# The first tile of rows for a mixture of experts: turned by TensorE from marks of the slots, with later row loads and turns moved within a tile

## The reference

```python
h = (x - mu) * jax.lax.rsqrt(var + LN_EPS) * ln_g + ln_b
logits = jnp.einsum('btd,ed->bte', h, w_r) + b_r
topk_vals, topk_idx = jax.lax.top_k(logits, K)          # K = 2 of 8
gates = jax.nn.softmax(topk_vals, axis=-1)
hid = jax.nn.gelu(jnp.einsum('nd,edf->nef', hf, W1) + b1, approximate=False)   # 512 -> 2048
expert_stack = jnp.einsum('nef,efd->ned', hid, W2) + b2                        # 2048 -> 512
# each row: its two experts' results, weighted by the gates, added to x
```

## Time and profile before

| what | value |
|---|---|
| time, median of 3 runs | 2133.72 us (2128.21 to 2137.45) |
| the profiled execution | 2126.98 us, of which 2125.2 us span |
| TensorE busy | 1715.3 us, 81% |
| VectorE, ScalarE, GpSimd busy | 919.6, 519.3, 875.1 us |
| granted TensorE clock, mean | 0.935 |

### The profile page before, as it was taken

How to read it: one execution, slowest core, us unless ns; L and a number is a source line. 1 busy time by engine, 2 the same in 40 slices (tenths; PEclk the granted TensorE clock), 3 DMA queues, 4 the chain that set the end, 5 groups by cost and what they waited for, 6 DMA issues and landing times. The chain is left out here.

```text
span 2125.2 us, 27922 instructions
## 1 busy us (share of the span) xinstructions
PE 1715.3 (81%) x8075; PEld 1126.1 (53%) x8076; DVE 919.6 (43%) x2223; ACT 519.3 (24%) x1459; POOL 875.1 (41%) x1032
## 2 busy tenths in 40 slices
PE   4649988756937777786879999279999999999992
PEld 4224434334436666652434465157777777777770
DVE  3852266344159999969845638400000000000001
ACT  0011101111138888820111122011222211122220
POOL 0677778777669999965011100220000000043002
PEclk9999998978969999998889999589999999999996
DMA  7900031000230000010210013543803320420003
GB/s 202 298 2 2 2 76 31 2 2 2 65 114 25 0 0 0 0 61 0 94 56 1 0 37 122 211 131 150 331 20 144 150 76 20 178 63 20 20 20 102
DMA packets 77073, 150.32 MB, mean 71 GB/s; under 512 B 19795, under 2 KB 21402, under 8 KB 72802
## 3 DMA queue, kind: packets, MB, share of 16 engines
q1 hardware_dynamic: 50533, 125.26, 16.5%
q0 software_dynamic: 19200, 11.30, 3.7%
q10 hardware_dynamic: 7294, 13.21, 1.8%
HBM read 111.35 MB, written 37.99 MB: 70 GB/s over the span
## 5 line engine op out<-in xcount | busy, mean ns | idle before, releaser
L310 POOL DMA_INDIRECT sorted_edges<-fa_records,fa_edge_slot x320 | 399.4, 1248 | 176.2 <-issue 176.2
L1838 PEld LDWEIGHTS et_ps_h<-et_turned,arena 128*128 128x128 f32 x3072 | 348.6, 193 | 19.2 <-issue 15.9
L1838 PE MATMUL et_ps_h<-et_turned,arena 128*128 128x128 f32 x3072 | 349.1, 276 | 7.6 <-issue 4.5
L1847 PE MATMUL et_ps_y<-arena,et_hidden_t 128*128 x768 | 333.6, 592 | 0.0
L909 POOL TENSOR_SCALAR ad_row<-iota,ad_row_no 128x128 fp32r<-128x128 f32 x354 | 237.9, 685 | 0.1
L1847 PEld LDWEIGHTS et_ps_y<-arena,et_hidden_t 128*128 128x128 f32 x768 | 144.0, 190 | 172.2 <-issue 172.2
L1749 POOL DMA_INDIRECT xn_rows<-slot_out,slots x10 | 12.2, 1218 | 493.8 <-POOLq L1746 491.0
L986 PE MATMUL ad_ps_w<-ad_to,ad_row_high 128*128 128x320 f32 x472 | 150.1, 330 | 63.5 <-POOL ad_row_low L914 60.5
L964 ACT ACTIVATE ad_row_high<-ad_row,ad_edges 128x128 fp32r<-128x128 f32 x472 | 184.5, 391 | 67.9 <-DVE ad_row L933 67.0
L1765 DVE COPY et_turned<-et_ps_t 128x512 f32<-128x512 f32 x25 | 17.3, 692 | 370.7 <-PE et_ps_t L1819 370.7
L931 DVE TENSOR_SCALAR ad_to<-iota,ad_edges 128x320 fp32r<-128x320 f32 x472 | 176.6, 433 | 0.0
(11 more groups left out here) (363 smaller groups left out, 2327.2 us busy)
## 6 DMA issues: line engine op xcount, KB each, us to landing
arena<-L_ffn_W SPq DMA_DIRECT2D x16, 4096.0 KB, 13.3
slot_rows<-fa_zeros SPq DMA_DIRECT2D x1, 7424.0 KB
slot_out<-fa_zeros SPq DMA_DIRECT2D x1, 6912.0 KB
et_rows_in<-slot_rows ACTq DMA_DIRECT2D x26, 256.0 KB, 2.6
slot_out<-et_y ACTq DMA_DIRECT2D x24, 256.0 KB, 2.0
sorted_edges<-fa_records,fa_edge_slot POOLq DMA_INDIRECT x320
x_in<-x SPq DMA_DIRECT2D x1, 2500.0 KB
neighbour<-fa_Wv SPq DMA_DIRECT2D x10, 250.0 KB
```

What stands on the lines that cost most here:

```text
L310: nc.gpsimd.indirect_dma_start(g.sorted_edges, bass.IndirectOffsetOnAxis(ap=self.edge_slot[0:NT, e:e + 1], axis=0), self.records[0:NT, e, ...
L1838: last = pe.matmul(ps_h[:, f % 2, i, :], x.weights[:, at:at + P], turned[:, k, :], start=(k == 0), stop=(k == KD - 1))
L1847: last = pe.matmul(ps_y[:], hidden_t[:, i, :], x.weights[:, bass.ds(buffer * (2 * HALF) + (HALF + i * D), D)], start=(i == 0), stop=(i == ...
```

## The change

It has three parts.

**Early and late scatters.** One list of twenty scatters, lower slots first. POOL issues the first seven (EARLY = 7) in nodes and does not wait for them; it issues the other thirteen in expert_tiles, behind the announcement of expert 0. All count on one semaphore, `rows_scattered`.

**The first tile without DRAM.** In nodes VectorE makes `marks`: for each node tile a 125x128 matrix with a 1 where a row's lower slot equals the column's number. TensorE multiplies the rows by the marks, 4 x 10 matmuls into one PSUM bank, which gives the rows of slots 0 to 127 turned. ScalarE copies the bank to `x.turned`, which lives on into expert_tiles (and holds the row `be` before that, whose buffer is dropped). No load, turn or copy of tile 0 is left in expert_tiles; TensorE gives the three semaphores their first counts there.

**Loads and turns in the loop.** ScalarE's queue loads the rows of tile t + 1 behind the Gelus of tile t, and TensorE turns them ahead of the last quarter of tile t's second product instead of ahead of its first.

```diff
+EARLY = 7
+def scatter_rows(nc, g, choices):
+    for i in choices:
+        n, t = divmod(i, T)
+        nc.gpsimd.indirect_dma_start(
+            g.slot_rows, bass.IndirectOffsetOnAxis(ap=g.slots[0:NT, n, t:t + 1], axis=0),
+            g.xn[0:NT, t, :], None).then_inc(g.rows_scattered, 16)
...
+        marks = sums[:, 2 * DST - T * P:].rearrange("p (t n) -> p t n", t=T)
...
@@ nodes, gpsimd
             pool.wait_ge(s["slots_ready"], 1)
-            for t in range(T):
-                nc.gpsimd.indirect_dma_start(
-                    g.slot_rows, bass.IndirectOffsetOnAxis(ap=g.slots[0:NT, 0, t:t + 1], axis=0),
-                    g.xn[0:NT, t, :], None).then_inc(g.rows_scattered, 16)
-            pool.wait_ge(g.rows_scattered, 16 * T)
+            scatter_rows(nc, g, range(EARLY))
@@ nodes, scalar
+            act.wait_ge(s["first_turned"], 1)
+            nc.scalar.copy(x.turned[:].rearrange("p k n -> p (k n)"), banks[:, 3, :])
@@ nodes, vector
+            c.link(v.tensor_tensor(least[r, :], chosen_slot[0][r, :], chosen_slot[1][r, :], ALU.min))
+            for t in range(T):
+                v.tensor_scalar(marks[r, t, :], g.iota[r, 0:P], column(least, t), None, ALU.is_equal).then_inc(s["marked"], 1)
@@ nodes, tensor
+            for k in range(KD):
+                for t in range(T):
+                    if k == 0:
+                        pe.wait_ge(s["marked"], t + 1)
+                    last = pe.matmul(banks[:, 3, k * P:(k + 1) * P], g.xn[r, t, k * P:(k + 1) * P], marks[r, t, :],
+                                     start=(t == 0), stop=(t == T - 1))
+            last.then_inc(s["first_turned"], 1)
@@ expert_tiles, gpsimd
             announce(0)
-            for t in range(T):
-                nc.gpsimd.indirect_dma_start(
-                    g.slot_rows, bass.IndirectOffsetOnAxis(ap=g.slots[0:NT, 1, t:t + 1], axis=0),
-                    g.xn[0:NT, t, :], None).then_inc(g.rest_scattered, 16)
+            scatter_rows(nc, g, range(EARLY, 2 * T))
@@ expert_tiles, vector
-            move_turned(0)
@@ expert_tiles, scalar
-            load_rows(0)
-
-            act.wait_ge(s["rows_turned"], 1)
-            act.wait_ge(g.rest_scattered, 16 * T)
-            load_rows(1)
...
-                act.wait_ge(s["rows_turned"], t + 2)
-                load_rows(t + 2)
+                act.wait_ge(g.rows_scattered, 16 * 2 * T)
+                act.wait_ge(s["rows_turned"], t + 1)
+                load_rows(t + 1)
@@ expert_tiles, tensor
-            turn_rows(0)
+            for n, amount in (("rows_loaded", 16), ("rows_turned", 1), ("rows_ready", 1)):
+                pe.sem_inc(s[n], amount)
...
-                turn_rows(t + 1)
                 pe.wait_ge(s["weights_ready"], e * 2 + 2)
                 pe.wait_ge(s["y_out"], t + 1)
                 for f in range(FC):
                     pe.wait_ge(s["hidden_ready"], t * FC + (f + 3))
+                    if f == FC - 1:
+                        turn_rows(t + 1)
```

More of the change, by code:

```diff
@@ L424, in __init__ @@
         self.scattered, self.rows_scattered = m.sem("scattered"), m.sem("rows_scattered")
-        self.rest_scattered = m.sem("rest_scattered")
         self.low_gathered, self.gathered = ([m.sem(f"{n}{t}") for t in range(T)] for n in ("low_gathered", "gathered"))
@@ L1005, in __init__ @@
         self.weights = arena
-        self.b1 = m.sb("b1", [P, EXPERTS * FT])
+        self.b1, self.turned = m.sb("b1", [P, EXPERTS * FT]), m.sb("turned", [P, KD, P])
         self.ends = m.sb("ends", [P, EXPERTS], I32)
@@ L1122, in nodes @@
         agg = m.sb("agg", [P, 2, GCN])
-        be = m.sb("be", [P, D])
+        be = x.turned[:].rearrange("p k n -> p (k n)")
         in_degree, degree, positive, guess, root_y, root_off = (
@@ L1147, in nodes @@
                  "q_ready k_ready dotted comp_in comp_ready agg_done agg_out value_ready out_done out_taken h_ready lifted rows_made "
-                 "logits_done picked counted odds_in odds2_ready slots_ready "
+                 "logits_done picked counted odds_in odds2_ready slots_ready marked first_turned "
                  "chain")
@@ L1183, in _ @@
             sp.dma_start(expert, A["L0_ffn_We"][bass.ds(e, 1)].squeeze(0).rearrange("(k p) n -> p k n", p=P)).then_inc(s["fetched"], 16)
-            sp.dma_start(be[:], A["L0_ffn_be"][bass.ds(e, 1)].squeeze(0).partition_broadcast(P)).then_inc(s["fetched"], 16)
+            sp.dma_start(be, A["L0_ffn_be"][bass.ds(e, 1)].squeeze(0).partition_broadcast(P)).then_inc(s["fetched"], 16)
             load_matrix(sp, wo, A["L1_mix_Wo"], s["rest_in"])
@@ L1687, in expert_tiles @@
         m = Memory(nc, stack, "et_")
-        turned, hidden_t = m.sb("turned", [P, KD, P]), m.sb("hidden_t", [P, FT, P])
+        turned, hidden_t = x.turned, m.sb("hidden_t", [P, FT, P])
         rows_in, y = m.sb("rows_in", [P, D]), m.sb("y", [P, D])
@@ L1741, in _ @@
             pool.wait_ge(s["weights_ready"], 2 * EXPERTS)
-            pool.wait_ge(g.rest_scattered, 16 * T)
+            pool.wait_ge(g.rows_scattered, 16 * 2 * T)
             low_end = pool.value_load(x.ends[0:1, EXPERTS - 2:EXPERTS - 1], min_val=0, max_val=SLOT_TILES)
@@ L1779, in load_rows @@
             def load_rows(t):
-                act.dma_start(rows_in[:], in_rows[t] if isinstance(t, int) else in_rows[bass.ds(t, 1)].squeeze(0)
-                              ).then_inc(s["rows_loaded"], 16)
-            load_rows(0)
-            act.wait_ge(s["rows_turned"], 1)
-            act.wait_ge(g.rest_scattered, 16 * T)
-            load_rows(1)
+                act.dma_start(rows_in[:], in_rows[bass.ds(t, 1)].squeeze(0)).then_inc(s["rows_loaded"], 16)
             with used_tiles(act) as t:
@@ L1804, in _ @@
             act.sem_inc(s["finished"], 1)
-            act.wait_ge(s["rows_loaded"], last_end(act) * 16 + 32)
+            act.wait_ge(s["rows_loaded"], last_end(act) * 16 + 16)
             act.sem_inc(s["finished"], 1)
```

## The result

The changed kernel took 2105.49 us (median of 4 runs, 2102.89 to 2111.30), the kernel before, run with it on the same chip, 2130.97 us (4 runs, 2123.45 to 2137.45). The ratio is 0.9888, with an interval of 0.9853 to 0.9923: 1.1% faster. A later series of 6 runs gave 2110.83 against 2129.17 (11 runs), 0.9906 [0.9877, 0.9934]. The forecast was 2116 us. Its profiled execution took 2105.39 us with a span of 2103.6, so 21.6 us less than the span of the profile before.

The account below looks back on a forecast made before the run. TensorE bounds the loop without idle time but stands almost still for 37 us ahead of it. Hand-over 14.4 plus first-tile stall 3.1 gives 17.5 us, from the 2133.72 median 2116 us, range 2106 to 2126.

Parts of the forecast that it names:

- The base: Whole kernel: 17.5 us gain measured from the runs' median, 2133.72 us, the profiled execution being 6.7 us faster.
- Early scatters: End of nodes: POOL's drain holds until seven scatters land; B, the barrier's opening, at 1374.0 to 1375.0 us, taken as 1374.5.
- the first rival: End of nodes: POOL's drain doesn't hold; TensorE and the copy set B at 1371.3, gain 20.8 us, 2113 us; chance 0.13.
- The entry: Start of expert_tiles: first pass at B + 5.4, between B + 4.2 and B + 6.8, with 0.7 us per register load.
- Marks and forty matmuls: In nodes: ten marks 3 us, matmuls from 1358.3 to 1369.2 or 1371.0; hidden by POOL, 2 to 4 us to spare.
- Both rivals about them: In nodes: clock stays at half, gain 14.7 us, chance 0.06; marks hold up scatters, gain 14.5 us, chance 0.07; each 2119 us.
- ScalarE at B: First tile: ScalarE enters its loop when the barrier opens, removing the wait before the third quarter; 3.1 us gained.
- Late scatters: First tile: thirteen land at B + 26.9, tile 1's rows loaded at B + 29.5, wanted at B + 32.2; 2.7 us to spare.
- The loop: Loop: loads 3 us and turned rows about 2 us to spare; seams bounded at 0.2 us a tile, taken as nothing.
- The slower rival: Loop: the turn in the last quarter misses each next tile's start; at 1.2 us late each, 2145 us; chance 0.04.

Follow-up runs that it names:

- e5: Changed kernel plus twenty more marks on VectorE into spare buffers, beside the early scatters; 2113.0 us (one run).
- e8: Changed kernel with EARLY = 6 and the turn ahead of the last three of sixteen blocks instead of the last four; 2109.57 us (one run).
- e3: Changed kernel with ten early scatters instead of seven (EARLY = 10); 2122.4 us.
- e6: Changed kernel with a semaphore wait on POOL for the seven early scatters, ahead of the drain at the end of nodes; 2105.02 us.
- e9: Kernel before, with its late scatters held until the first quarter of the first product is done; 2142.64 us.
- e4: Changed kernel with three early scatters instead of seven (EARLY = 3); 2108.28 us.
- e1: Kernel before with only the changes in the loop, none at the hand-over; 2122.76 us (8 runs), ratio 0.9966 to the kernel before.
- c1: Kernel before, traced once more without a change; 2127.77 us.
- e2: Changed kernel's hand-over with the loop of the kernel before; 2131.32 us (10 runs), ratio 1.0004 to the kernel before.
- c2: Changed kernel, traced once more without a change; 750.7 us from S, the start of the slots instruction, to the end.
- e10: Changed kernel with EARLY = 5 and the turn ahead of the last three of sixteen blocks; 2106.08 us (6 runs), ratio 0.9892 to the kernel before.
- e7: Changed kernel with 28 unread matmuls (twelve ending nodes, sixteen starting expert_tiles) in TensorE's gap; 755.2 us from S, the slots instruction's start, to the end.

## Why the prediction came out as it did

The mechanism is the forecast's: POOL's drain holds the barrier, nothing in the loop is lost, and the gain is in the hand-over and the first tile. The gain was 18.9 and 19.9 us behind S in two pairs of traces, where 17.5 was forecast. The time of 2105.49 us lies half a microsecond below the low end of the forecast, 2106; the ratio of the runs side by side, applied to 2133.72, gives 2109.8.

- **The base.** The forecast was measured from a median of three runs, 2133.72. The same kernel gave 2130.97, 2130.04 (17 runs) and 2129.17 (11 runs), and 2123.93 beside the single runs of e5 to e8. Of the 10.5 us between 2116 and 2105.49 some 3 to 4 are this, 1.4 to 2.4 are the larger gain, and the other 5 are the draw of the runs: the changed kernel's own second series was 5.3 us slower than the first. From 2130 the forecast's own sum would have given 2112.5, 1.7 us from the 2110.83 of the second series.
- **Early scatters: B at S + 17.0, measured 16.0 and 16.8.** The step holds. A drain waits for the landing (e3, e6); it ends 5.0 and 5.8 us behind the seventh's issue, where 5.5 for the landing and 0.4 to 1.1 for the drain were taken. So the first rival (POOL's drain doesn't hold) is out.
- **The entry, mis-sized.** B + 5.4 was forecast, B + 4.45 measured. Its step was "I take 0.7 each" for the register loads: they took 0.47, 0.32 and 0.32. The 1.2 us of before came from the late scatters beside them (e9), and in the changed kernel, at the last of its loads, the first late scatter was only just being issued (1373.44 and 1374.2 us). With 1.1 us for the three instead of 2.1 the sum gives B + 4.4.
- **Marks and forty matmuls: 10.9 to 12.7 us, measured 11.96**, with 27 slow passes (0.215 us) ahead of fast ones (0.112). The turn is hidden behind POOL, as forecast, with 2.5 us to spare; with three early scatters turn and copy set the barrier (e4, S + 13.3 against 12.7). A mark took 0.28 us by itself, as the earlier trace rows had it, but marks overlap: the ten took 2.31 us, not 3. Both rivals about them are out: the clock rose, and a scatter beside marks lost 0.04 us.
- **ScalarE at B: 3.1 us.** The stall is gone. The first tile gave 3.7 in the first pair: 3.3 from the stall and its surroundings (e1) and 0.3 from 3.1 instead of 3.8 us at half clock. In the second pair it gave 6.4, for c1's stall was 4.38 us and the clock fell back around it. And 3.1 hides what e2 shows: without this edit the loss would be 18.97, because the late scatters land 27.6 us behind B, and the first pass stands only 4.45 us behind it.
- **Late scatters: 2.7 us to spare, measured about none.** The step "landed at B + 26.9 ... B + 5.4 + 26.8 = B + 32.2" failed in size. They landed at B + 27.6, the load was issued at once and had its rows there at B + 30.4, and TensorE would have begun on them at B + 30.2, because entry and first product were 1.0 and 0.5 us shorter and the weights of a transpose are loaded ahead of it. The wait stayed hidden behind the passes under way. In c2, where the clock rose later, there is none; in e5 the matmuls waited 0.56 us.
- **The loop: spare of 2 to 3 us, seams at nothing.** Right: the period went from 28.463 to 28.466 us, and a turn ahead of the last three of the sixteen matmuls (e8, e10) leaves it at 28.466 too, but for the one tile of e10. The slower rival is far off.

What is left to gain at this place is bounded by POOL. One scatter fewer ahead of the barrier opens it up to 1.5 us earlier and puts one more, 1.5 us, behind it, so with five to ten early scatters the last late one is issued by S + 37.6 to S + 38.8 all the same. The rows of tile 1 then come between S + 45.9 and S + 48.7: 46.4, 48.1 and 45.9 with seven (the changed kernel, e5, e6), 46.0 with six, 47.4 with five, so that one trace each doesn't tell these splits apart. With three the turn and the copy hold the barrier, the last late scatter is issued by S + 41.2, and the rows come at S + 49.3. An earlier first pass runs into these rows.

## What to carry to other kernels

An early start of one engine is worth what the next engine in the chain allows: the hand-over alone gained nothing (e2), since ScalarE's queue still held a wait for the late scatters ahead of its loop, so look for waits ahead of a loop that only its later turns need. A block that ends with DMAs in flight on GpSimd ends when they have landed, so how many are issued there is a price in time, and how many are left for later is another; find where the two meet. When a forecast of half a per cent is wanted, take the base from many runs of before and count from an event close ahead of the change.

## What the runs showed of the hardware

- GpSimd's drain at a block's end holds for its scatters, from ahead of their issue to 0.6 to 0.8 us behind their last packet: 12.5, 13.7, 14.4, 15.6 (16.4 in c2) and 20.5 us with three, five, six, seven and ten, 0.63 us where a wait had already seen them land (e6).
- A scatter of 125 rows of 2 KB: the drain ends 5.0 and 5.8 us behind the issue of the seventh and 7.9 us behind that of the third (S + 4.8 to S + 12.7, e4). In that stretch the changed kernel's DMA share stands at 1.02 to 1.04. By the packets of their queue, taken in order, scatters end 3.7 to 7.5 us behind their issue in the fourteen traces. The Trainium skill (DMA: Bandwidth & Descriptors, Anatomy of one DMA — SWDGE (gpsimd) path) has about 2.0 us plus the bytes; no scatter here was that fast.
- Beside each scatter's issue two VectorE operations of 0.27 us take 0.58 and 0.45 us, and the scatter 0.04 us more (e5).
- A register load on TensorE takes 0.30 to 0.50 us, but 0.70 to 1.50 beside late scatters (before, c1, e1), and 2.22 behind fillers (e7).
- Filler matmuls did not hold the clock over the entry: it fell at S + 23.5 instead of S + 16.8, and the first pass came at S + 25.0 (e7). In the changed kernel, one program, it rose at S + 23.6 in one execution and S + 27.0 in another, which is 1.2 us in the first product.
